# Start, block-to-block passages and experts' entry and exit reordered in a one-core adaLN + RWKV + mixture-of-experts kernel

## The reference

```python
mod = (silu(c) @ wmod).reshape(4, 6, 1, 512)
sa, ca, ga, sb, cb, gb = (mod[:, i] for i in range(6))
ga = (2 * (ga >= 0) - 1) * maximum(abs(ga), 0.25)      # gb likewise
h = layernorm(x) * (1 + ca) + sa
# attention part on h: layer norm 1, shift in time, k, v, r = mixes @ Wk, Wv, Wr
#   wkv from exp(k), v;  h += sigmoid(r) * wkv @ Wo
#   layer norm 2, shift, kv = silu(mix @ Wkey) @ Wval; sr = sigmoid(mix @ Wcr); h += sr * kv
x = x + ga * attention(h)
h = layernorm(x) * (1 + cb) + sb
# experts on h: two shared ones (gelu(h @ up) @ down), softmax router over 16 experts, top 2
x = x + gb * (shared(h) + routed(h))
```

## Time and profile before

| what | us |
|---|---|
| median of 3 runs | 942.76 |
| lowest and highest | 938.45, 944.33 |
| span of the profiled execution | 937.6 |
| PE busy | 892.2 |
| DVE busy | 529.4 |
| ACT busy | 383.2 |
| POOL busy | 381.2 |

### The profile page before, as it was taken

How to read it: one execution, slowest core, us unless ns; L and a number is a source line. 1 busy time by engine, 2 the same in 40 slices (tenths; PEclk the granted TensorE clock), 3 DMA queues, 4 the chain that set the end, 5 groups by cost and what they waited for, 6 DMA issues and landing times.

```text
span 937.6 us, 13563 instructions
## 1 busy us (share of the span) xinstructions
PE 892.2 (95%) x4264; PEld 719.0 (77%) x4265; DVE 529.4 (56%) x999; ACT 383.2 (41%) x632; POOL 381.2 (41%) x282
## 2 busy tenths in 40 slices
PE   7899869999998999999999999999999999999996
PEld 2457658878776888788888888888877888888875
DVE  5897797988667111274327432742486444444488
ACT  2557565573736533322232223215452333333352
POOL 2332200100022446416301630167815599998573
PEclk9899989999998999999999999999999999999999
DMA  9548578566046426876212521267353789876887
GB/s 357 192 129 255 199 231 256 158 203 203 23 157 209 144 97 206 243 239 209 91 34 72 198 90 34 87 203 282 114 157 124 247 248 278 279 247 223 260 252 194
DMA packets 121824, 174.03 MB, mean 186 GB/s; under 512 B 8216, under 2 KB 69656, under 8 KB 118704
## 3 DMA queue, kind: packets, MB, share of 16 engines
q1 hardware_dynamic: 58896, 111.55, 34.9%
q0 software_dynamic: 9216, 34.61, 12.1%
q10 hardware_dynamic: 53664, 27.26, 9.9%
HBM read 97.58 MB, written 75.81 MB: 185 GB/s over the span
## 4 chain that ended last, share of the span: by engine, by line
PE 71%; DVE 12%; DMA 5%; issue 4%; ACT 3%; POOL 3%; SPq 1%; DVEq 0%; ACTq 0%
PE kk_ps L425 6%; PE kk_ps L427 6%; PE kk_ps L426 6%; PE kv_ps L425 6%; PE kv_ps L427 6%; PE kv_ps L426 6%; PE mm_ps L425 4%; PE mm_ps L426 4%; PE mm_ps L427 4%; PE up_ps L425 3%; PE dn_ps L425 3%; PE dn_ps L427 3%; PE dn_ps L426 3%; PE up_ps L426 2%; PE up_ps L427 2%
## 5 line engine op out<-in xcount | busy, mean ns | idle before, releaser
L1563 DVE TENSOR_TENSOR silu<-kk_ps,silu 128x512 fp32r<-128x512 f32 x64 | 44.2, 691 | 196.5 <-ACT silu L2229 196.2
L2225 ACT ACTIVATE kk_ps<-kk_ps 128x512 f32<-128x512 f32 x64 | 37.2, 582 | 206.5 <-PE kk_ps L427 206.5
L425 PE MATMUL kk_ps<-xk,cm_w 128*128 128x512 f32 x256 | 100.9, 394 | 2.3 <-DVE xk L1608 2.3
L425 PE MATMUL kv_ps<-cm_w,silu 128*128 128x512 f32 x256 | 100.6, 393 | 0.0
L427 PE MATMUL kk_ps<-xk,cm_w 128*128 128x512 f32 x256 | 99.8, 390 | 0.0
L427 PE MATMUL kv_ps<-cm_w,silu 128*128 128x512 f32 x256 | 99.7, 390 | 0.0
L426 PE MATMUL kk_ps<-xk,cm_w 128*128 128x512 f32 x256 | 99.6, 389 | 0.0
L426 PE MATMUL kv_ps<-cm_w,silu 128*128 128x512 f32 x256 | 99.6, 389 | 0.0
L2393 POOL TENSOR_TENSOR cm_w<-stage,cm_w 128x1024 fp32r<-128x1024 f32 x16 | 38.7, 2423 | 90.5 <-ACT cm_w L2013 74.7
L2400 POOL TENSOR_TENSOR rs<-mv,neghalf 128x4 f32<-128x4 f32 (+2 forms) x13 | 13.8, 1065 | 144.1 <-DVE mv L1274 144.0
L1890 DVE TENSOR_TENSOR xsT<-xs_ps,xsT 128x512 fp32r<-128x512 f32 x42 | 28.9, 691 | 73.9 <-ACT xsT L2310 73.9
(11 more groups left out here) (297 smaller groups left out, 2361.6 us busy)
## 6 DMA issues: line engine op xcount, KB each, us to landing
xs_s<-zero ACTq DMA_DIRECT2D x13, 1024.0 KB, 6.1
ys_s<-zero ACTq DMA_DIRECT2D x13, 1024.0 KB, 6.3
xsb<-xs_s SPq DMA_DIRECT2D x44, 256.0 KB, 3.8
ys_s<-ysb SPq DMA_DIRECT2D x41, 256.0 KB, 3.4
ex_raw<-in_wex POOLq DMA_DIRECT2D x9, 1024.0 KB, 6.3
stage<-in_wcm SPq DMA_DIRECT2D x16, 512.0 KB, 3.7
wmod<-in_wmod SPq DMA_DIRECT2D x6, 1024.0 KB, 11.8
ex_raw<-in_wex SPq DMA_DIRECT2D x6, 1024.0 KB, 8.0
```

What stands on the lines that cost most here:

```text
L425: pe.matmul(out, lhs[0], rhs[0], start=first, stop=False)
L1563: dve.tensor_tensor(silu[:, g % NSILU, 1, :], kk_ps[g % 2][:, :], silu[:, g % NSILU, 0, :].bitcast(F32), ALU.subtract).then_inc(s_silo, 1)
L2225: act.activation(kk_ps[g % 2][:, :], kk_ps[g % 2][:, :], ACT.Silu).then_inc(s_silu, 1)
```

## The change

All products are the same ones; order, waits and one integer type change.

- SP: the load of x's first four tiles goes ahead of `wmod[0]`.
- PE: `modulation(2)` goes behind the transposes of sequence 0, `modulation(5)` behind the first K tile. ACT: `rows_out(2)` goes between the second and third `mixed_hi("K", 0)`, `rows_out(5)` between the second and third `mixed_hi("V", 0)`. DVE: `gate_floor(2)` goes from before the first `differences` to just before `gate_floor(5)`, with a wait between.
- POOL: `weight_lo(0)` waits for `first_norm_c(0)`, `weight_lo(1)` for `nm2`; at the entry of the experts the four `post_rsqrt` go ahead of `weight_lo(34)` and `weight_lo(35)`.
- ACT: no `clear_slots` in g = 14 to 16; the six left are issued in g = 17 to 22.
- Entry: `shared_up(1, [2])` ahead of `table_row`; ACT's Exp behind `gelu(1)`; DVE's `mid_lo(4)` ahead of `table_b`, `mid_lo(5)` ahead of `gb_shared(1)`, `table_d` ahead of `mid_lo(6)`, `gb_shared(4)` ahead of the gates.
- Exit: half of the first tile of `shared_up(2)` goes ahead of the last `down`.
- The table of expert tiles is uint16 and not int32.

```diff
-        tab = sbuf(top, "tab", [1, 2, NSX], I32)
+        tab = sbuf(top, "tab", [1, 2, NSX], U16)
...
-            for i in (1, 0):
-                sp.dma_start(wmod[:, i], wmod_d[i]).then_inc(s_wmod[i], 16)
+            sp.dma_start(wmod[:, 1], wmod_d[1]).then_inc(s_wmod[1], 16)
...
             load_x(0)
+            sp.dma_start(wmod[:, 0], wmod_d[0]).then_inc(s_wmod[0], 16)
             load_tm(0)
...
             first_rows(1)
             first_rows(0)
-            for i in range(3):
+            for i in range(2):
                 modulation(i, mm_ps[i])
-            modulation(5, mm_ps[3])
             turn_by_tile(1, 0, [0, 1])
             turn(1, 0, [2, 3])
+            modulation(2, mm_ps[2])
...
                     channels_out("K", b, [m])
+                    if b == 0 and m == 0:
+                        modulation(5, mm_ps[3])
...
-            def shared_up(b, tiles=range(KT)):
+            def shared_up(b, tiles=range(KT), blocks=range(KT)):
...
-                    for k in range(KT):
+                    for k in blocks:
...
-                    mm.then_inc(s_up, 1)
+                    if KT - 1 in blocks:
+                        mm.then_inc(s_up, 1)
...
-            shared_up(1, [0, 1])
+            shared_up(1, [0, 1, 2])
             table_row()
-            shared_up(1, [2, 3])
+            shared_up(1, [3])
...
+            shared_up(SB, [0], range(2))
             down(slot_of(pe.snap(kept[0], min_val=0, max_val=8 * NE - 1)), 0, pairs * 2 + 1, pairs * 2 + 1)
+            shared_up(SB, [0], range(2, KT))
...
-                shared_up(b)
+                shared_up(b, range(b == SB, KT))
...
-            gate_floor(2)
             differences(1, 0, [0, 1])
...
                     r_out(b, 1)
+                    gate_floor(2)
+                    dve.wait_ge(s_ke, 2)
                     gate_floor(5)
...
             table_a()
+            mid_lo(4)
             table_b()
             table_c()
+            mid_lo(5)
             gb_shared(1)
-            mid_lo(4)
             gb_shared(2)
-            mid_lo(5)
+            table_d()
+            mid_lo(6)
             gb_shared(3)
-            mid_lo(6)
             mid_lo(7)
-            table_d()
+            gb_shared(TT)
             gates_b()
             by_expert()
             last_tiles()
-            gb_shared(TT)
...
-            for i in range(3):
+            for i in range(2):
                 rows_out(i, mm_ps[i])
             hn_out(1, 0)
-            rows_out(5, mm_ps[3])
             act.wait_ge(s_bc, 32)
             to_hT(1, 0)
-            mixed_hi("K", 0)
+            mixed_hi("K", 0, [0, 1])
+            rows_out(2, mm_ps[2])
+            mixed_hi("K", 0, [2, 3])
             weight_hi(2)
             weight_hi(3)
-            mixed_hi("V", 0)
+            mixed_hi("V", 0, [0, 1])
+            rows_out(5, mm_ps[3])
+            mixed_hi("V", 0, [2, 3])
...
-                elif 18 + g - 12 < len(groups):
+                elif g < 14:
                     clear_slots(18 + g - 12)
+                elif 17 <= g < 23:
+                    clear_slots(20 + g - 17)
...
+            gelu(1)
             act.wait_ge(s_sub, 1)
             act.activation(pr[:, :, :], pr[:, :, :], ACT.Exp).then_inc(s_exp, 1)
-            gelu(1)
...
             rsqrt(rs1, mv1, 0, s_st1, s_rs1, 0)
+            pool.wait_ge(s_h0, TT)
             weight_lo(0)
             rsqrt(rs2, mv2, 0, s_st2, s_rs2, 1)
+            pool.wait_ge(s_nm2, 1)
             weight_lo(1)
...
             ht_lo(0)
+            for t in range(NT - TT, NT):
+                post_rsqrt(t)
             weight_lo(34)
             weight_lo(35)
-            for t in range(NT - TT, NT):
-                post_rsqrt(t)
             scatters(NB - 1)
```

More of the change, by code:

```diff
@@ L16 @@
 I32 = mybir.dt.int32
+U16 = mybir.dt.uint16
 ALU = mybir.AluOpType
@@ L557, in _ @@
             sp.dma_start(cT[:, :, :], c_d).then_inc(s_small, 16)
-            for i in (1, 0):
-                sp.dma_start(wmod[:, i], wmod_d[i]).then_inc(s_wmod[i], 16)
-            nx = [0]
+            sp.dma_start(wmod[:, 1], wmod_d[1]).then_inc(s_wmod[1], 16)
             def load_x(b, tiles=range(TT)):
@@ L1085, in _ @@
             last_values()
-            def shared_up(b, tiles=range(KT)):
+            def shared_up(b, tiles=range(KT), blocks=range(KT)):
                 for m in tiles:
                     n = b * KT + m
[L1090 to L1099, removed]
-                    for k in range(KT):
+                    if 0 in blocks:
+                        if n >= 2:
+                            pe.wait_ge(s_midlo, n - 1)
+                        else:
+                            pe.wait_ge(s_silo, NB * MF)
+                        if m == 0 and b == SB:
+                            pe.wait_ge(s_txhi, pairs * 2 + 2)
+                            pe.wait_ge(s_txlo, pairs * 2 + 2)
+                        if n == 0:
+                            pe.wait_ge(s_whi, 28)
+                            pe.wait_ge(s_wlo, 28)
+                    for k in blocks:
                         if m == 0:
```

## The result

The median fell from 942.60 us (6 runs, 938.22 to 948.16) to 933.32 us (6 runs, 929.22 to 937.47); ratio 0.991, 95% interval 0.988 to 0.9939. A second series of the changed kernel gave 935.89 us against 940.72, ratio 0.9937 (0.9913 to 0.9961). The forecast was 938.0, a fall of 4.8. The medians of the two series fell by 9.3 us (interval 5.7 to 11.3) and by 4.8 (3.7 to 8.2). The profiled execution has a span of 930.4 us against 937.6 of before, 7.2 less.

The account below looks back on a forecast made before the run. PE, busy 892.2 of 937.6 us, was taken as the bound, except at the very start and end; 0 + 0 + 2.3 + 2.5 + 0 = 4.8 us off the 942.76 median gave 938.0, range 933.5 to 942.5.

Parts of the forecast that it names:

- The verdict it gave the most weight: Whole kernel: the time stays within one percent, 9.4 us, of the kernel before; chance 0.89.
- The sign named for the right case: Entry of the experts: no PE waits for t_ps and up_ps, and the loop starts 4.8 us earlier.
- Norms' chain: Start, DVE's norms to ACT's hn: two operations no longer overlapped by POOL's, about 4.0 us won, hn near 23.1.
- What PE gives back: First sequence: moved modulations stand in PE's way, modulation(2) mostly at half clock; V at 50.8; taken 0, bounds -0.5 to +1.1.
- Gate rows and the rest of phase 1: Second gate_floor costs 2.3 more, an earlier r_out offsets it; taken 0, bounds -2.3 to +1.1; later phase 1 untouched.
- Passage: First passage between sequences in phase 2: without the clears xkr lands sooner, PE's wait goes; 2.3 us, bounds 1.0 to 2.4.
- Entry: Entry of the experts: PE's waits of 1.03 and 1.54 go; taken 2.5 us, bounds 0.7 to 2.6.
- Exit: End: PE's 1.13 wait is filled, but POOL's upper gather sets the end; taken 0, bounds -0.3 to +1.1.
- Sum: Whole kernel: 0 + 0 + 2.3 + 2.5 + 0 = 4.8 us gained, giving 938.0; chance 0.47.

Follow-up runs that it names:

- e9: The changed kernel without POOL's two waits at the start (weight_lo(0) and weight_lo(1) as early as before): 939.16 us, ratio 0.996 to the kernel before.
- e5: The kernel before with the uint16 table alone: 941.97 us, ratio 0.9997 to the kernel before.
- e8: The changed kernel with tiles 1 to 6 combined one at a time on DVE instead of in pairs: 932.20 us, ratio 0.9901 to the kernel before.
- e12: The changed kernel with e8's single tiles, two upper gathers sooner, and DVE and ACT work moved ahead at the exit: 932.80 us, ratio 0.99 to before.
- e11: The changed kernel with POOL's low parts 34 and 35 ahead of post_rsqrt again: 935.08 us, ratio 0.9932 to the kernel before.

## Why the prediction was right, and where its terms were off

The verdict it gave the most weight, a gain too small for one percent, held, and the sign too, but narrowly and partly by luck: the first series fell by 9.3 us where one percent is 9.4, almost twice the forecast, and its median of 933.32 lies 0.2 below the range's lower end of 933.5. The second series fell by just the 4.8 of the forecast, while three of the terms behind that number were off. The sign named for the right case, the loop starting 4.8 us earlier, read 10.8 in after's first trace and 6.6 in its second. By term, with what the traces give on average in place of the forecast's number:

- **Norms' chain: right.** 4.0 forecast; `hn` moved by 3.9 (27.08 to 23.18), and e9 takes it back. The mechanism, DVE held by POOL's low parts, is the one in the trace. What the Trainium skill ("SBUF — State Buffer", section "Who interferes with whom") says of operations with one SBUF input agrees with the trace: four statistics took 2.46 us with a low part beside them, and 2.46 us without one in before.
- **What PE gives back: mis-sized.** "I take half clock for most of it": `modulation(2)` took 4.56, not 6.3, because the granted clock was half (1.2 GHz) only for its first 2.0 us and full (2.4 GHz) for the rest of it. V at 49.88 is thus near the 49.6 that the prediction gave for the full clock. V came 0.5 us sooner on average, not 0.1 later.
- **Gate rows and the rest of phase 1: the step that failed**, the gate rows "Taken: 0" and, from there on, "nothing is touched, and whatever this stage gives passes on". After V another 1.6 us came on average. The gate rows went with V: `gate_floor(5)` started 1.1 sooner in after's trace (78.61 to 77.49), V 0.8 sooner. The rest came behind them. At 190 us the seven traces with the moved products and POOL's waits are 1.7 us ahead of before's on average, from 2.9 ahead to 0.9 behind (after's second), and the six with the products in their old place 0.1. Behind 190 us before's own trace has its stretch at half clock, which no row of a single trace could tell to be rare. The start as a whole gave about 2.1. How much of it is order and how much the clock isn't settled.
- **Passage: mechanism right, size off.** 2.3 forecast from one trace whose wait was the longest of five; with the clears moved the passage is 1.4 shorter on average.
- **Entry: right, mis-sized by 0.6.** 2.5 forecast, 2.8 to 3.3 measured, 3.1 on average. `post_d(15)` was held for one POOL operation, as taken, and cost PE nothing.
- **Exit: right, by the wrong picture.** 0 forecast and 0 found: with the exit's edit and tiles in pairs it is 3.1 us over before's trace on average (six traces), without it 3.2 (five, before's own 0 among them). But the forecast said that what ends the kernel is the gather that DVE waits for at 894.48; in most traces it is an upper gather behind the stretched ones, some 20 us later. The trace of before does not have them.
- **Sum.** 2.1 + 1.4 + 3.1 + 0 = 6.6 us, against 4.8 forecast and 9.3 (interval 5.7 to 11.3) and 4.8 (3.7 to 8.2) measured in two series. Both intervals hold 6.6.

## What to carry to other kernels

When a change is worth less than one percent, profile the old kernel several times before pricing stalls: here one trace had a wait of 2.3 us that is 1.2 on average, and lacked the stretched gathers (6.8 us longer in e5) that ten of the eleven other traces with paired tiles have. A pair of edits can be worth something only together (the norms sooner, the products out of their way): look at what stands next in each engine's queue before you price one alone. And where POOL issues gathers beside DVE, a DVE queue without pauses may be slower than one with them (e8).

## What the runs showed of the hardware

- POOL's DMA_INDIRECT takes 0.96 us, and 2.77, 3.43 and 3.43 us in most traces (two or three gathers in ten of twelve) while DVE works through combining steps in pairs without a pause; the excess of 1.81 and 2.47 is near three and four of DVE's steps (0.60 to 0.66 apart). Beside DVE operations with pauses of 0.03 us between them the rows of e8 have 1.08 to 1.14, and no gather of e8's or e12's exit took over 1.46. That it is the pauses that remove it rests on these two traces and on e8's time. Two of the twelve traces with pairs (before, e11) have no stretched lower gather either, and why is open. In these two a pair of tiles took DVE 3.79 us, as long as three gathers of 1.26, and in the others 3.73; whether gathers in step with DVE find their places isn't tested.
- A DVE operation held by POOL's back-to-back low parts was held over both when it came 1.2 us into the first (4.11 and 4.12 us; 4.11 to 4.15 in all six traces with the old order), and over the first alone when it came 0.14 us into it (2.79 us; 2.78 to 2.81 in all eight with the new one). What decides isn't known.
- The granted clock's half stretches in the first 310 us differ from execution to execution of the same code: 13.7 us in all in after's first trace, 17.1 in its second. Before's trace has 27.3, the most of all, and e5's, which differs from it only in the table's type, 20.5. The first of them was 3.4 us long in all seven traces with waits and moved products and 6.8 or more in the others.
